# The head norm's weight moved from the normalised value to the gate, and onto GpSimd

## The reference, cut to what matters

```
h   = o * hs                                   # o: sigmoid gate, hs: output of the recurrence
hn  = (h - mean) * rsqrt(var + eps) * mh_g + mh_b    # per head of 64
out = (hn + x_skip) * silu(r_t)
y   = out @ W_down.T + b_down + x
```

## Time and profile before

| what | value |
| --- | --- |
| median of three runs | 448.0 us (445.31 to 449.13) |
| the profiled execution: its time and span | 448.0 us |
| TensorE matmuls busy | 383.7 us, 86% |
| vector engine busy | 342.7 us, 77% |
| ScalarE busy | 225.4 us, 50% |
| GpSimd busy | 125.8 us, 28% |
| chain that ended last | issue 41%, TensorE 23%, vector engine 18%, GpSimd 9% |
| mean granted TensorE clock | 0.958 of full speed |

### The profile page before, as it was taken

One profiled execution on the slowest core, in us unless ns is written; L12 is line 12 of the kernel. 1 busy time (PEld: TensorE's weight loads), 2 busy tenths in 40 slices (PEclk: granted clock), 3 DMA queues, 4 the chain that ended last, 5 costly groups with the idle time before them and its releaser, 6 DMA issues.

```text
span 448.0 us, 11432 instructions
## 1 busy us (share of the span) xinstructions
PE 383.7 (86%) x3623; PEld 302.6 (68%) x3645; DVE 342.7 (77%) x1061; ACT 225.4 (50%) x591; POOL 125.8 (28%) x125
## 2 busy tenths in 40 slices
PE   8166999999998899898899898899888967879991
PEld 5022999945876677776668676678667843669991
DVE  4883577766649989869989689999699997658870
ACT  3731444425465565455584455475555641455650
POOL 5574244511003101111110121111021138544552
PEclk9669899999999999999999999999999987999996
DMA  7996122159999999999500000000000612333320
GB/s 217 368 411 177 39 72 71 54 147 168 168 166 158 169 162 166 153 150 159 102 1 0 0 0 0 0 0 0 1 1 1 233 53 83 108 99 91 88 78 2
DMA packets 57265, 46.11 MB, mean 103 GB/s; under 512 B 4111, under 2 KB 53905, under 8 KB 56721
## 3 DMA queue, kind: packets, MB, share of 16 engines
q1 hardware_dynamic: 53618, 37.84, 41.8%
q0 software_dynamic: 2752, 5.73, 3.7%
q10 hardware_dynamic: 864, 2.15, 1.6%
HBM read 17.99 MB, written 27.25 MB: 101 GB/s over the span
## 4 chain that ended last, share of the span: by engine, by line
issue 41%; PE 23%; DVE 18%; POOL 9%; ACT 3%; DMA 3%; DVEq 1%; POOLq 0%; SPq 0%; another core or an unknown queue 0%; ACTq 0%
PE bank L896 21%; POOL HS L567 5%; POOL slots L519 3%; PE bank L1033 1%; DVE ST L1419 1%; ACT WVT L786 1%; ACT E L795 1%; POOL LA L561 1%; DMA XN<-slots 1%; DVE W1R L2006 1%; DVE OUT L2044 1%; DVE W1R L2008 1%; DVE W1R L2005 1%; DMA QKT<-by_token 1%; DMA slots<-XN,POS 1%
## 5 line engine op out<-in xcount | busy, mean ns | idle before, releaser
L567 POOL TENSOR_TENSOR HS<-HS,MHALF 128x8 f32<-128x8 f32 x16 | 26.3, 1646 | 148.2 <-DVE HS L1999 148.2
L786 ACT ACTIVATE WVT<-bank,AC 128x128 f32<-128x128 f32 x128 | 36.6, 376 | 29.0 <-PE bank L896 29.0
L896 PE MATMUL bank<-XBT,W1R 128*128 128x128 f32 x368 | 50.6, 282 | 0.2 <-ACT XBT L689 0.2
L896 PE MATMUL bank<-W,HT 128*128 x368 | 49.0, 276 | 1.6 <-issue 1.6
L896 PEld LDWEIGHTS bank<-XBT,W1R 128*128 128x128 f32 x368 | 45.8, 196 | 1.0 <-ACT XBT L689 0.6
L896 PEld LDWEIGHTS bank<-W,HT 128*128 128x128 f32 x368 | 44.8, 192 | 2.3 <-issue 2.0
L696 ACT ACTIVATE HT<-bank,W1R 128x128 f32<-128x128 f32 x115 | 34.8, 366 | 16.6 <-PE bank L896 10.9
L896 PE MATMUL bank<-MASKB,IDB 128*128 128x512 bf16 x130 | 35.6, 400 | 4.9 <-POOL HS L567 3.2
L519 POOL DMA_INDIRECT slots<-XN,POS x32 | 32.2, 1006 | 18.7 <-issue 8.7
L750 ACT ACTIVATE QKT<-bank,COLS 128x512 f32<-128x512 f32 x32 | 22.0, 687 | 26.5 <-PE bank L896 26.5
L1953 DVE TENSOR_TENSOR WOT<-bank,WVT 128x512 f32<-128x512 f32 x32 | 21.9, 685 | 14.7 <-ACT WVT L786 14.7
(11 more groups left out here) (360 smaller groups left out, 983.6 us busy)
## 6 DMA issues: line engine op xcount, KB each, us to landing
slots<-FILL SPq DMA_DIRECT2D x74, 258.0 KB
W<-w SPq DMA_DIRECT2D x2, 2048.0 KB, 10.6
XN<-slots SPq DMA_DIRECT2D x23, 129.0 KB
W<-w SPq DMA_DIRECT2D x1, 2064.0 KB
slots<-QKT SPq DMA_DIRECT2D x1, 1483.5 KB, 6.8
XB<-slots SPq DMA_DIRECT2D x23, 64.5 KB
X<-x SPq DMA_DIRECT2D x4, 256.0 KB, 5.3
QKT<-by_token SPq DMA_DIRECT2D x4, 256.0 KB, 4.1
```

The source lines that it names most:

```text
L567: g.tensor_tensor(HS[:, 3, :], HS[:, 2, :], MHALF[:, 0:H], ALU.pow).then_inc(roots_ready, 1)
L786: ins = a.activation(DT[:, hf, m, :], DM[:, m * P:(m + 1) * P], ACT.Exp, bias=AC[:, c, h:h + 1])
L896: return t_.matmul(o, l, r, start=start, stop=stop, skip_group_check=True)
```

## The change

On GpSimd a new function `addends(b, c)` waits until the skip and the gate of a chunk have been evicted and writes SK[c] = SK[c] * GR[c], then GR[c] = GR[c] * mhg, with a wait between them. Its four calls stand among the roots. The vector engine then computes (centred value * root) * GR[c] + SK[c] in three passes, and waits for `addend_ready` ahead of the second. The last chunk of the last batch keeps its own order on the vector engine, but takes its addend and its scaled gate from GpSimd too. The waits of the vector engine for the two evictions go, and `hn_ready` with them.

```diff
--- before.py
+++ after.py
@@ -326,9 +326,10 @@
         tanh_ready, xc_ready, rows_ready = sem("tanh_ready"), sem("xc_ready"), sem("rows_ready")
         rth_ready, m3_ready = sem("rth_ready"), sem("m3_ready")
         dm_full, dm_free, st_full, pt_ready = sem("dm_full"), sem("dm_free"), sem("st_full"), sem("pt_ready")
+        skip_gated = sem("skip_gated")
         hv_full, hv_read, cs_ready, qs_ready = sem("hv_full"), sem("hv_read"), sem("cs_ready"), sem("qs_ready")
         cen_ready, sq_ready, hvar_ready = sem("cen_ready"), sem("sq_ready"), sem("hvar_ready")
-        hn_ready, outg_ready = sem("hn_ready"), sem("outg_ready")
+        addend_ready, outg_ready = sem("addend_ready"), sem("outg_ready")


         PJ = bank[0:2]
@@ -566,13 +567,25 @@
                 pool.wait_ge(hvar_ready, b * NC + c + 1)
                 g.tensor_tensor(HS[:, 3, :], HS[:, 2, :], MHALF[:, 0:H], ALU.pow).then_inc(roots_ready, 1)

+            def addends(b, c):
+
+                pool.wait_ge(*pj_read_at(b, f"s{c}"))
+                pool.wait_ge(*pj_read_at(b, f"r{c}"))
+                g.tensor_tensor(SK[c], SK[c], GR[c], ALU.mult).then_inc(skip_gated, 1)
+                pool.wait_ge(skip_gated, NC * b + c + 1)
+                g.tensor_tensor(GR[c], GR[c], row("mhg", HID), ALU.mult).then_inc(addend_ready, 1)
+
             def sequence(b, last):
+                addends(b, 0)
                 if not last:
                     norms(b + 1)
                 else:
                     rstd(1, 0)
+                addends(b, 1)
                 roots(b, 0)
+                addends(b, 2)
                 roots(b, 1)
+                addends(b, 3)
                 if not last:
                     roots(b, 2)
                     roots(b, 3)
@@ -1806,7 +1819,7 @@
                 do(v.tensor_copy(SKIPB[64:65, :], SK23[0:1, 0, :]))
                 v.memset(CREDIT[:, 11:12], 0.0).then_inc(skip_bias_ready, 1)
                 for i, s in enumerate((*pj_free, tr_free, xc_ready, pt_ready, dm_free, hv_read,
-                                       outg_ready, hn_ready, qs_ready)):
+                                       outg_ready, qs_ready)):
                     v.memset(CREDIT[:, i:i + 1], 0.0).then_inc(s, 1)
                 v.memset(MIN[:, :], 0.0).then_inc(attn_consts, 1)
                 dve.wait_ge(attn_consts, 1)
@@ -2003,25 +2016,13 @@
                 dve.wait_ge(roots_ready, NC * b + c + 1)
                 flat = H2[:, :, :].rearrange("p h d -> p (h d)")
                 do(v.tensor_tensor(H2[:, :, :], H2[:, :, :], bc(HS[:, 3, :], [P, H, HD]), ALU.mult))
-                do(v.tensor_tensor(flat, flat, row("mhg", HID), ALU.mult))
-                dve.wait_ge(*pj_read_at(b, f"s{c}"))
-                v.tensor_tensor(flat, flat, SK[c], ALU.add).then_inc(hn_ready, 1)
-
-            def last_addend(b):
-
-
-                dve.wait_ge(*pj_read_at(b, "r3"))
-                dve.wait_ge(*pj_read_at(b, "s3"))
-                did(v.tensor_tensor(SK[3], SK[3], GR[3], ALU.mult))
-
-            def last_gate_scale():
-
-                step.settle()
-                did(v.tensor_tensor(GR[3], GR[3], row("mhg", HID), ALU.mult))
-
-            def last_scale():
+                dve.wait_ge(addend_ready, NC * b + c + 1)
+                did(v.tensor_tensor(flat, flat, GR[c], ALU.mult))
+
+            def last_scale(b):

                 flat = H2[:, :, :].rearrange("p h d -> p (h d)")
+                dve.wait_ge(addend_ready, NC * b + 4)
                 step.settle()
                 did(v.tensor_tensor(flat, flat, GR[3], ALU.mult))

@@ -2036,12 +2037,11 @@

             def gate(b, c):

-                dve.wait_ge(hn_ready, b * NC + c + 2)
-                dve.wait_ge(*pj_read_at(b, f"r{c}"))
+                step.settle()
                 if c:

                     dve.wait_ge(*tr_full_at(b, f"o{c - 1}"))
-                v.tensor_tensor(OUT[:, :], H2[:, :, :].rearrange("p h d -> p (h d)"), GR[c], ALU.mult)\
+                v.tensor_tensor(OUT[:, :], H2[:, :, :].rearrange("p h d -> p (h d)"), SK[c], ALU.add)\
                  .then_inc(outg_ready, 1)

             def update_x(b, c):
@@ -2061,9 +2061,7 @@
                 else:
                     take_k(b, 0)
                 if last and c == 3:
-                    last_addend(b)
                     weigh(b, 3, 1)
-                    last_gate_scale()
                     scale_q(b, 3)
                     early_choice()
                 if c >= 2:
@@ -2115,7 +2113,7 @@
                     early_full()
                 variance(b, 3)
                 if last:
-                    last_scale()
+                    last_scale(b)
                     early_experts()
                 else:
                     gate_copies(b + 1)

```

## The result

The changed kernel takes 455.26 us (455.0 to 455.27, four runs), the kernel before 447.43 us (445.31 to 449.13, four runs). The ratio is 1.0175 with a 95% interval of 1.0135 to 1.0215. Run again beside other kernels it took 454.08 against 446.44 us, 1.0152 (1.0093 to 1.0212). The times in this document are medians of all executions of a kernel; the ratios leave out four slow ones (one of the kernel before, one of ten with the multiplies placed, two of ten with them halved), which ran at a lower granted clock than the others of their kernel and over 1.5% above its fastest.

A forecast was written before the change was run, and what follows sets the result against it. TensorE and the vector engine, both nearly full, were taken to bound the kernel. Saved passes and blocks net +5.4 over three batches and +2.0 in the last, +7.4 on 448.0: 455 us, range 440 to 459.

The forecast's parts named there:

- the two waits of TensorE: Chunk 1's k transposes wait 1.27 us, the batch's last gated output 1.07; saved passes give -1.79 per batch.
- Blocking both ways, whole passes long: GpSimd multiplies and vector passes with two SBUF inputs stop each other for whole passes; 455 us, chance 0.59.
- a root of 1.45 us against one of 1.00: Same-shape input-norm roots on GpSimd: the first, beside a two-input vector pass, took 1.45 us; taken as GpSimd waiting.
- the QS pass inside a root: Two-input vector pass during chunk 0's root kept its usual 0.68 us: evidence against blocking; the root reads only 8 elements.
- The blocks, chunk by chunk: Net per batch: chunk 0 +0.4, chunk 1 +1.4, chunk 2 +1.05, batch end -1.07; +1.8, three batches +5.4.
- the model of the interface: GpSimd and two-input vector passes exclude each other at SBUF; called wrong if one-input passes stretch or multiplies take 2 us.
- The last batch: Up to the slot numbers: +0.1 in chunk 0, +1.5 each in chunks 1 and 2, -1.2 for moved passes; +2.0.
- The gain of -2.6: Last batch without blocking: -0.72 x 2 for passes in chunks 1 and 2, -1.20 for two moved to GpSimd.
- all of it counts up to the slot numbers: In the last batch TensorE has no projections to hide behind, so all saved time counts until the scatter's release; -2.6.
- No blocking: Rival: GpSimd's multiplies yield or interleave and only they get longer; sum -8.0, 440 us, chance 0.26.
- Half blocking: Rival: interface held for half the multiply, or vector engine wins ties in chunks 1 and 2; 447.7 us, chance 0.12.
- late behind its neighbour's multiplies: Rival: multiplies over 2.4 us delay chunk 0's root in GpSimd's in-order queue; 465 us and more at 3 each, chance 0.03.

The follow-up runs named there:

- the multiplies placed: Changed kernel with GpSimd's multiplies released where almost no two-input vector pass runs, last batch's chunk 3 left as before; 441.23 us, 0.9888 of before.
- halved: Changed kernel with each GpSimd multiply cut into two of 256 columns; 448.33 us, 1.0026 of before.
- 8 columns: Changed kernel with each of the 32 GpSimd multiplies cut to 8 of 512 columns, same waits and order; 441.44 us, 0.9871 of before.
- memsets: Changed kernel with two 128x516 memsets and three 8-column multiplies in place of each GpSimd multiply; 440.93 us, 0.9889 of before.
- reading without any other change: Kernel before plus 32 GpSimd multiplies from constant rows into an unused tile, vector engine untouched; 466.30 us, 1.0434 of before.

## Why the prediction held

- **Which engines bound the kernel, and where.** Right. With the blocks away (8 columns) a batch gained 1.96 us where the forecast from the two waits of TensorE was 1.79, and the waits that were left were those worked out.
- **Blocking both ways, whole passes long.** Right, and shown four ways: no reading, no cost (8 columns, memsets); reading without any other change, +19.9 us; the same reading at other moments, hardly a cost (a batch of 62.49 us against 62.34 with 8 columns). The forecast rested on a root of 1.45 us against one of 1.00 and a stretched copy, and it set aside the QS pass inside a root. That reading of the QS row was right too: with 8 columns the root's and the gate's product stay within 684 to 694 ns.
- **The blocks, chunk by chunk.** To the residual update of chunk 1 (L2055, 217.66 - 197.74 = 19.92 us into the batch) the changed kernel had lost 1.84 us, forecast 0.4 + 1.4. To that of chunk 2 (232.39) it had lost 2.88, so 1.04 more, forecast 1.05. The end gave 1.25 back, forecast 1.07. Which passes are hit in chunk 1 was right for the first and the third batch, and for all three of the repeated run. In the second batch, whose times the forecast used, it came out one pass later, because the skip's copy was late there. The cost was the same, 1.84 against 1.79 lost up to L2055 in the first batch.
- **The price of a multiply.** 1.27 us alone, 1.15 assumed, within 0.95 to 1.38; 1.60 where it comes second, within the 1.8 given.
- **A sign that the forecast named against itself.** "If passes with one SBUF input are stretched too" the model of the interface is wrong, it says. One kind is: the scaling of 8 numbers in chunk 0, 0.41 us for 0.17. The large passes with one SBUF input aren't. So the model held for what decides the time, and is incomplete.
- **The last batch.** Its sum was right, +2.4 for +2.0, but by two errors. The gain of -2.6 was too large: with 8 columns the stretch to the 128x4 root is 54.27, only 1.2 less than 55.47. The 1.44 of chunks 1 and 2 is there: the first weighing of chunk 3 comes 25.92 us behind the 128x12 root instead of 27.35. The two passes moved away brought nothing. With 8 columns it takes 3.30 us from this weighing to the reduction behind the QS pass (349.35 to 352.65), before the change 3.00 (357.17 to 360.17). In place of the two passes the vector engine waits for ScalarE's exponentials, 0.38 us in front of the second weighing and 0.93 in front of QS:

```profile
350.42 0.69 DVE L1966 TENSOR_TENSOR WOT<-bank,WVT 128x512 f32<-128x512 f32 x1 [0.38 <-ACT WVT L799]
352.04 0.69 DVE L1973 TENSOR_TENSOR QS<-QKT,E 128x512 f32<-128x512 f32 x1 [0.93 <-ACT E L808]
```

  Neither waited for anything in the kernel before. The step "all of it counts up to the slot numbers" failed here: what would be late next was looked for on TensorE alone. (With memsets the stretch is 55.52, as long as before; TensorE's granted clock was 0.88 over its first 13.87 us there, with 8 columns 1.00, and the vector engine waited 0.75 us for TensorE.) The blocks there were smaller too, 3.6 us by the difference of 57.83 and 54.27 where the forecast had some 4.6. So the right sum of this batch is luck.
- **The sum.** +7.4 against +7.1 in the trace and +7.8 in the times. Without blocking -8.0 was forecast, -7.1 is what the trace with 8 columns gives and -5.8 its ratio (0.9774 to 0.9968, that is -1.4 to -10.1).
- **What it was laid upon.** The forecast took the profiled execution's 448.0 for its time. That is its span; in the profiled executions of the other kernels the time is 2.1 to 3.2 us more (changed kernel: 455.0 for 451.8). The time of that execution of before isn't on record; by this difference it is estimated at 450.1 to 451.2, some 3 above the median, about the 3.25 by which its first expert layer was longer than in the changed kernel's. The sum was laid on the median, so this did the number no harm, but that the profiled execution stood at the median is very likely wrong.
- **The rivals.** No blocking (440) is refuted by the stretched passes, though it is the time of a kernel in which they don't meet. Half blocking (447.7) is refuted by the same passes; that the halved multiplies took about that time, 448.33, is chance. No root was late behind its neighbour's multiplies: the smallest gap in front of one was 2.42 us in the loop and 0.54 in the last batch, apart from the last root, which the scatter holds as before.

The Trainium skill, "SBUF — State Buffer", section "Who interferes with whom", had the mechanism: two SBUF inputs on the vector engine against a GpSimd instruction that reads. The trace agrees for whole instructions of 512 and 256 elements (1.71 for 0.69, 1.22 for 0.69), and for memsets, which don't read, it agrees that nothing is stopped. It doesn't agree that the whole instruction counts for a GpSimd one of 8 elements: QS kept its 0.68 inside a root of 1.64.

## What to carry to other kernels

In these runs elementwise work that reads SBUF on GpSimd held up the vector engine's passes with two SBUF inputs, and not its large passes with one. Before moving such work, count the overlap with its two-input passes at the full length of the GpSimd instruction, in both directions, and compare that with the pass saved: here 0.69 us saved against two multiplies of 1.27. Before dropping such a move, look for stretches in the vector engine's order where one large input comes from PSUM, and release the GpSimd work by the semaphore that opens the stretch: here that turned +1.5 to +1.75% into -1.1% (0.9857 to 0.9919). And ask of each saved pass which engine is late next: the two taken from the last batch only uncovered a wait for ScalarE.

## What the runs showed of the hardware

- A GpSimd multiply of 128x512 in float32 with both inputs in SBUF takes 1.27 us, one of 256 columns 0.73, one of 8 columns 0.20 where nothing holds it up, a copy of 128x512 0.60, a memset of 128x516 0.52 to 0.53.
- The multiply of 8 x 128 numbers by a constant on the vector engine (L2005), with one SBUF input, was stopped as well: 0.41 us for 0.17 in chunk 0, ending with the multiply (203.13 and 203.10). The sum over 128x512 just ahead of it, also with one SBUF input, was not. So the count of SBUF inputs alone doesn't decide; no run here took the two apart further.
  The section of the Trainium skill named above has both: it counts the operations of the scaling's kind among those that can also take the pair of ports shared with GpSimd, and a sum among those that on this chip never contend.
- The extension is put on the pass that waits, as busy time: the vector engine's share rose from 77% to 78% while it did 17 passes less. A group whose mean lies far above that of a like group (1696 against 692 ns) is the sign to look for.
- The first expert layer varied between 97.3 and 100.6 us among profiled executions with the same instructions. TensorE's granted clock over it doesn't order them (0.90 at 100.56 us, 0.91 at 97.31, 0.88 at 97.32). Its cause is open.
